# Layer 0 of a four-layer graph network: the neighbour sum of the graph before is turned over behind the shared slots' gathers instead of in front of their seeds

## The reference, cut to what matters

```python
mask = (adj > 0.0)
W1a, W1b = W1[:F], W1[F:]
xj_proj = x @ W1a
diff = x[:, :, None, :] - x[:, None, :, :]
h = relu(xj_proj[:, :, None, :] + diff @ W1b + b1)     # every pair of nodes (j, k)
hm = einsum('bjkh,bjk->bjh', h, mask)                  # sum over the neighbours k
return hm @ W2 + deg[..., None] * b2
```

## Time and profile before

| what | value |
|---|---|
| time, median of 3 runs | 1491.98 us (1490.49 to 1494.42) |
| profiled execution | 1490.96 us, span 1489.0 us |
| PE matmul busy | 1322.7 us, 89% of the span |
| DVE busy | 1171.4 us, 79% |
| ACT busy | 1113.2 us, 75% |
| POOL busy | 496.4 us, 33% |
| mean granted clock of TensorE | 0.970 of full speed |

### The profile page before, as it was taken

How to read it: one execution, slowest core, us unless ns; L and a number is a source line. 1 busy time by engine, 2 the same in 40 slices (tenths; PEclk the granted TensorE clock), 3 DMA queues, 4 the chain that set the end, 5 groups by cost and what they waited for, 6 DMA issues and landing times. The chain is left out here.

```text
span 1489.0 us, 41572 instructions
## 1 busy us (share of the span) xinstructions
PE 1322.7 (89%) x11243; PEld 1077.9 (72%) x11244; DVE 1171.4 (79%) x3091; ACT 1113.2 (75%) x2424; POOL 496.4 (33%) x611
## 2 busy tenths in 40 slices
PE   0799999999999999999999999997999997972298
PEld 0477777777777777777777777775888887920298
DVE  6598898988888889888898898985444445978755
ACT  0788888888888888888888888883555554916676
POOL 0143344443343344443343344442112221057400
PEclk9999999999999999999999999998999998986599
DMA  7000000000000000000000000000000000000022
GB/s 150 15 9 9 15 7 7 7 13 8 7 7 7 14 7 7 7 13 9 7 7 7 14 7 7 0 2 1 1 0 0 0 0 0 0 1 0 2 55 56
DMA packets 40926, 18.11 MB, mean 12 GB/s; under 512 B 19573, under 2 KB 40887, under 8 KB 40887
## 3 DMA queue, kind: packets, MB, share of 16 engines
q1 hardware_dynamic: 40354, 17.42, 4.8%
q10 hardware_dynamic: 532, 0.21, 0.1%
HBM read 13.44 MB, written 4.19 MB: 12 GB/s over the span
## 5 line engine op out<-in xcount | busy, mean ns | idle before, releaser
L833 DVE SCALAR_TENSOR_TENSOR acc<-slot_banks,acc 128x768 f32<-128x768 f32 x512 | 486.7, 951 | 43.0 <-PE slot_banks L555 32.5
L901 POOL TENSOR_TENSOR acc<-acc 128x384 f32<-128x384 f32 x128 | 128.2, 1002 | 562.2 <-DVE onediff L827 557.6
L555 PE MATMUL slot_banks<-ac_hi,work 128*128 128x192 f16 x1408 | 264.4, 246 | 1.0 <-ACT slot_banks L719 1.0
L555 PE MATMUL slot_banks<-ac_lo,work 128*128 128x192 f16 x1408 | 263.9, 246 | 0.0
L555 PE MATMUL slot_banks<-ac_hi,onediff 128*128 128x192 f16 x1024 | 186.1, 247 | 19.2 <-DVE acc L833 15.1
L555 PE MATMUL slot_banks<-ac_lo,onediff 128*128 128x192 f16 x1024 | 184.9, 246 | 0.0
L555 PEld LDWEIGHTS slot_banks<-ac_hi,work 128*128 (+1 forms) x1408 | 137.3, 98 | 62.5 <-issue 43.4
L555 PEld LDWEIGHTS slot_banks<-ac_lo,work 128*128 (+1 forms) x1408 | 138.0, 98 | 14.9 <-issue 6.3
L815 DVE TENSOR_SCALAR work<-work,slot_key 128x1024 f16 x256 | 119.6, 478 | 25.8 <-issue 25.8
L712 ACT ACTIVATE work<-slot_banks 128x576 f32<-128x576 f32 x128 | 83.4, 651 | 68.9 <-PE slot_banks L555 68.9
L555 PEld LDWEIGHTS slot_banks<-ac_hi,onediff 128*128 x1024 | 104.0, 102 | 41.4 <-issue 38.1
(11 more groups left out here) (261 smaller groups left out, 3308.5 us busy)
## 6 DMA issues: line engine op xcount, KB each, us to landing
adj_in<-in_adj_dram SPq DMA_DIRECT2D x32, 256.0 KB, 2.8
out_dram<-acc SPq DMA_DIRECT2D x32, 128.0 KB, 2.0
l1w<-in_L_gnn_W_dram SPq DMA_DIRECT2D x2, 64.0 KB
l1b<-in_L_gnn_b_dram SPq DMA_DIRECT2D x2, 64.0 KB
x_all<-in_x_dram SPq DMA_DIRECT2D x4, 0.2 KB, 12.1
nm_in<-in_nodemask_dram ACTq DMA_DIRECT2D x1, 64.0 KB
w1a<-in_L_gnn_W_dram ACTq DMA_DIRECT2D x1, 48.0 KB
w1b<-in_L_gnn_W_dram ACTq DMA_DIRECT2D x1, 48.0 KB
```

The lines of the kernel that those rows point to most:

```text
L555: last = nc.tensor.matmul(unit(pair, t, 1), hot(t), part[:, q, H:2 * H].unsqueeze(1), start=False, stop=(e == 1 and (t % SB == SB - 1 or t ...
L833: nc.vector.scalar_tensor_tensor(out=sums, in0=unit((q + k) % 2, 0, SU), scalar=0.0, in1=sums, op0=ALU.min, op1=ALU.add).then_inc(s_free[k ...
L901: nc.gpsimd.tensor_tensor(acc[:, q, 0:2 * H], acc[:, q, 0:2 * H], acc[:, q, 2 * H:4 * H], ALU.add)
```

## The change

In `pe_slots` a new function `behind` is called after the last shared gather, and `pe_transpose_sum` of graph b-1 moves from `between` into it. On ACT the two copies of a turned sum (`act_sum`) move from near the end of a graph's instructions to behind `act_seed`, and so are those of graph b-2 rather than b-1. One more `act_sum` follows the loop.

```diff
-        def pe_slots(pe, b, g, u, q, regs, first_done, halfway, between):
+        def pe_slots(pe, b, g, u, q, regs, first_done, halfway, between, behind):
...
             pe_gathers(q % 2, SS, lambda t: onehot2[:, t * N:(t + 1) * N], q).then_inc(s_done2, 1)
+            behind()
...
                     def between():
-                        if not (known(b) and b < 1):
-                            pe_transpose_sum(pe, b - 1, *group_of(b, g, u, q, 1))
                         if nxt is not None:
...
-                    pe_slots(pe, b, g, u, q, regs, first_done, halfway, between)
+                    def behind():
+                        if not (known(b) and b < 1):
+                            pe_transpose_sum(pe, b - 1, *group_of(b, g, u, q, 1))
+
+                    pe_slots(pe, b, g, u, q, regs, first_done, halfway, between, behind)
...
                         act_shared(act, b - 1, (q + 3) % GS)
                         act_seed(act, b, q)
+                    if not (known(b) and b < 2):
+                        act_sum(act, b - 2, *group_of(b, g, u, q, 2)[1:])
                     if q == 0 and not (known(g) and g == 0):
                         act_host_slots(act, g, u)
...
                     if q == 3 and not (known(g) and g + 2 >= NG):
                         act_h(act, g + 2)
-                    if not (known(b) and b < 1):
-                        act_sum(act, b - 1, *group_of(b, g, u, q, 1)[1:])
                     if nxt is not None and q == 3:
                         act_host_ranks(act, nxt, p)
...
                 act_shared(act, B - 1, 3)
+                act_sum(act, B - 2, 1, 2)
                 act_sum(act, B - 1, 1, 3)
```

## The result

The changed kernel takes 1535.49 us (median of 4 runs, 1534.71 to 1537.62) against 1491.24 us (4 runs, 1490.06 to 1494.42) before: 1.0291 times as long, 95% interval 1.0272 to 1.0311. The forecast was 1551, range 1515 to 1573. The profiled execution took 1535.34 us, its span 1533.4.

What follows compares the result with a forecast made beforehand. TensorE and DVE were taken to hand the bound to each other inside every group. 16 x (2.16 + 1.68) = 61 us, less 2 plus 1, gave 60 on 1490.96: 1551 us, range 1515 to 1573.

Steps and rivals of the forecast that it cites:

- the milder rival: Layer 0: AC's bank and the mask are in time, only the displaced block costs, 24 us, so 1515; chance 0.24.
- the rest of q=3 is DVE's chain: Layer 0, q=3: second half another 0.61 us late, everything after it shifts with DVE; group 2.16 us longer.
- The block ahead of q=0's seeds: Layer 0, TensorE: the turning block, now behind the shared gathers, makes q=0's seeds 0.70 us late.
- The wait for bank 6: TensorE's AC product of graph b+2 waits for ACT's two copies of b-2's turned sum: 0.27 us a graph.
- what would show it: L513 waits for ACT L725 in nearly every graph; DVE's L555 waits grow 0.4 to 1 us; group 32.4 us.
- the sum by that rule: AC and the turned sum share a bank; by the rotation rule alone, 128 stalls of 0.27, 35 us.
- The mask: ACT at q=0: copies put in front push the mask by 0.55 us, delaying TensorE's degree matmuls and shared seeds.
- The back edge: Every second group: the block covers the loop's branch, group 1.68 us longer; if not covered, 8 us more.
- Faster: Layer 0: ACT's seed holds the second half and begins earlier; up to 0.2 us a graph, 26 us, 1465; chance 0.07.
- No change: Layer 0: DVE is the bound everywhere, TensorE 0.45 us ahead at each hand-over; 1491; chance 0.05.

Runs made afterwards that it cites:

- the two pairs of edits: On the changed kernel: ACT's sum copied ahead of the seed plus one host-slot copy of three, 1518.64 us; sum copied first plus DVE's comparisons moved, 1497.04 us.

## Why the prediction was right

The direction was right and the time lies in the range, 15.5 us below the forecast. That it still fits is in part luck: the room below the forecast was there for the milder rival, and the term that came out smaller is another one. The walk through a group can be held against the trace event by event, in us after the half sum of q=3 (510.90 before, 531.99 after); the rows are worked out from the same starts and ends of DVE's L833 and L834.

| event | before | predicted | after |
|---|---|---|---|
| second half's sum of q=0 starts | 4.30 | 5.28 | 5.29 |
| half sum of q=0 ends | 6.75 | 7.71 | 7.74 |
| second half's sum of q=1 starts | 11.98 | 13.32 | 13.31 |
| half sum of q=1 starts | 13.25 | 14.81 | 14.83 |
| half sum of q=2 ends | 21.62 | 23.17 | 23.21 |
| second half's sum of q=3 starts | 26.29 | 28.45 | 28.51 |
| half sum of q=3 starts | 29.17 | 31.33 | 30.93 |
| the group | 30.12 | 32.28 | 31.87 |
| the group with the back edge | 30.75 | 32.43 | 31.94 |

**The mis-sized term.** Up to the second half's sum of q=3 no event is off by more than 0.06. Then "the rest of q=3 is DVE's chain", which I moved as a whole: from that sum to the half sum it took 2.88 before and takes 2.42 after. The 0.46, 32 times, are 14.7 of the 15.5 us. The chain holds the four comparisons, and shifted in time they meet less of POOL's instruction. In the row at 529.64 above only the first is stretched, to 0.54 us; it ends at 530.18, and POOL's instruction, the same as above, ended at 530.13. Over the kernel:

```profile
L804 DVE TENSOR_SCALAR work<-row,end 128x128 f16<-128x128 f16 x128 | 32.8, 316 | 0.1
```

Before, it was this:

```profile
L803 DVE TENSOR_SCALAR work<-row,end 128x128 f16<-128x128 f16 x128 | 48.5, 439 | 0.1
```

The 123 ns between the means, 128 times, are 15.7 us. The runs with the comparisons moved confirm that their place has a price (a mean of 251 or 252 ns, 13 and 8 us gained).

**The block ahead of q=0's seeds:** right. The seeds at 534.08 are 2.09 after the half sum (predicted 2.15), and its price, with the new wait and two of the copies ahead of the mask gone, is 28.6 us of layer 0 in a kernel of 1518.64 us; the milder rival, which held this alone, put it at 24 and 1515. What the prediction didn't see is that this price hangs on DVE being late at q=3.

**The wait for bank 6:** predicted 0.27, measured 0.31 at q=0, with the copies done and seen 2.58 after the last shared gather (535.70 less 533.12), predicted 2.60. The run with ACT's part alone shows the wait in the open, and in the runs with the sum copied first it is gone (the AC product starts 0.08 after the last gather). The sentence on what would show it was wrong, though: I wrote that without a wait on L513 the item is false, and the waits list only 1.4 us. Starts have to be read, not idle times. The rule of the Trainium skill (Perfetto Trace Analysis, section "Matmuls") that independent matmul groups should rotate through the banks spoke against the change, and the runs agree: the stalls add up to 35.2 us, as the sum by that rule had it, but they cost layer 0 only 9.5 to 20.1 us.

**The mask:** degrees at 539.62, that is 7.63 (predicted 7.66), shared seeds at 8.17 (8.19). The time was right and the cause half right. ACT's queue does push the mask, but with two of the three host-slot copies out of its way it is as late, since TensorE's adjacency transposes stand behind the delayed second half.

**The back edge:** the sum assumed that the branch is covered, and it nearly is. TensorE's timeline across it, with the half sum at 500.05, to be held against the earlier trace rows:

```profile
501.17 0.25 PE L555 MATMUL slot_banks<-ac_lo,work 128*128 128x192 f16 x1
501.25 0.38 PE L527 MATMUL bank<-ident,acc 128*128 128x128 f32 x2
...
501.92 0.39 PE L532 MATMUL bank<-work,hm 128*128 128x128 f32 x2
502.20 0.33 PE L548 MATMUL slot_banks<-ac_hi,ident 128*128 128x384 f16 x1
```

The seeds start 0.28 after L532, and where there is no back edge 0.22 after it (533.86 to 534.08). Of the 0.56 in the earlier trace rows some 0.06 are left (0.28 less 0.22), so the 8 us that stood in the range did not come.

**The rivals.** "Faster" needed ACT's seed to hold the second half; TensorE's list of waits in the changed kernel has none for that seed. "No change" needed DVE to be the bound everywhere; its waits for gathers rose by 57 us.

**The expectations missed** were of one kind: for ACT's part alone, TensorE's part alone, one host-slot copy, the two pairs of edits and, more narrowly, the sum copied first and the comparisons moved on the changed kernel, I added or cut terms as if each kept its size. In these runs, where two engines hand the bound to each other, a delay was swallowed, or passed on, by what stood there at that moment.

## What to carry to other kernels

Work that stands in front of a wait for another engine is free as long as that engine is the later one. Moved away, it has to be paid for, and so have the readers of its output, the buffer that it lies in and what is queued behind both (here 28.6, 9.5 and 8.1 us). When one instruction of several alike takes four times as long, look at what the neighbouring engine starts in that moment; moving it may gain more than the change under study (here four instructions moved gained 0.5%). And where undoing one cause shows nothing, undo a pair: two limits that coincide hide each other.

## What the runs showed of the hardware

- A small fp16 DVE comparison stands still while a POOL instruction runs that started first: 0.95 us for 0.24, from 508.30 to 509.25, POOL's from 508.29 to 509.21. The price depends on the phase between the two engines: 439 ns in the mean before, 316 after, 403 with the sum copied first, 250 with ACT's part alone, 252 moved. The Trainium skill (SBUF — State Buffer, section "Who interferes with whom") says that DVE in its two-port modes and GpSimd share a pair of ports, and that whoever issues first has it for the whole instruction; the two ends, 0.04 us apart, agree.
- A loop's back edge cost TensorE 0.56 us of idle time with nothing queued ahead of the seeds (0.80 us from the last gather to the seeds, against 0.32 at the end of a group without a back edge), and about 0.06 with a block of 0.9 us there. So the branch seems to be passed while the queued matmuls run; no record shows the branch itself.
- A wait of about 0.3 us in 124 graphs, 35.2 us from start to start, was listed as 1.4 us in 9, since a gather's record overlaps what follows by 0.17 us and the 0.14 left are too short for the list.
